# A hand-ordered drain with paired second norms and its own PSUM banks, and weight pieces converted one step sooner

## The reference

```python
h = x.as_patches @ W                                  # (64 images, 36 tokens, 192)
n = layernorm(h)
q, k, v = split(n @ W_attn.T + b_attn)                # 12 heads of 16
att = softmax(where(causal, q @ k.T / 4, -inf))       # 36 x 36 for each image and head
h = h + (att @ v) @ W_o.T + b_o
n = layernorm(h)
probs = softmax(n @ router_w.T)                       # 8 experts
top_w, top_i = top_k(probs, 2); top_w /= top_w.sum()
for e in range(8):                                    # 192 -> 768 -> 192
    h = h + w_e * (gelu(n @ w1[e] + b1[e]) @ w2[e] + b2[e])   # w_e: top_w of the tokens that chose e
```

## Time and profile before

| | us |
|---|---|
| median of three runs | 411.71 (411.45 to 411.98) |
| the profiled execution's own time | 414.29 |
| its span in the trace | 412.5 |
| PE busy in the span | 370.5 (90%) |
| DVE busy | 253.5 (61%) |
| ACT busy | 217.1 (53%) |
| POOL busy | 180.3 (44%) |
| granted TensorE clock, mean | 0.979 of full |

### The profile page before, as it was taken

One profiled execution on the slowest core, in us unless ns is written; L12 is line 12 of the kernel. 1 busy time (PEld: TensorE's weight loads), 2 busy tenths in 40 slices (PEclk: granted clock), 3 DMA queues, 4 the chain that ended last, 5 costly groups with the idle time before them and its releaser, 6 DMA issues.

```text
span 412.5 us, 14891 instructions
## 1 busy us (share of the span) xinstructions
PE 370.5 (90%) x5740; PEld 327.1 (79%) x5740; DVE 253.5 (61%) x656; ACT 217.1 (53%) x443; POOL 180.3 (44%) x219
## 2 busy tenths in 40 slices
PE   3989999989999999997998889999999999999900
PEld 3879989979989899874454589999999999999800
DVE  4696468877877778785298154555445555445425
ACT  5668667778787786853233144444444444444300
POOL 8116322246455452317308545555555555553300
PEclk9999999999999999999999999999999999999965
DMA  8974004433344333361151213121223222121167
GB/s 255 311 252 150 15 21 127 134 87 102 97 119 116 81 86 92 109 186 32 51 130 50 59 31 89 55 86 57 80 61 88 80 60 84 55 58 42 38 254 274
DMA packets 29705, 42.82 MB, mean 104 GB/s; under 512 B 12416, under 2 KB 19440, under 8 KB 29640
## 3 DMA queue, kind: packets, MB, share of 16 engines
q1 hardware_dynamic: 25512, 33.37, 26.9%
q0 software_dynamic: 4128, 8.50, 7.4%
HBM read 30.23 MB, written 9.67 MB: 97 GB/s over the span
## 4 chain that ended last, share of the span: by engine, by line
PE 41%; issue 6%; DVE 5%; POOL 3%; DMA 3%; ACT 1%; SPq 0%; POOLq 0%; DVEq 0%
PE PSA L1259 19%; PE PSA L1274 15%; PE PSA L1137 3%; DMA W2h<-yrows 3%; POOL XF L477 2%; PE PSA L1278 2%; PE PSA L1226 2%; DVE PTR L938 1%; DVE H L1000 1%; POOL REG L484 1%; DMA yrows<-KBR 1%; DVE VB L935 1%; POOL REG L483 1%; PE PSA L1204 0%; SPq L444 0%
## 5 line engine op out<-in xcount | busy, mean ns | idle before, releaser
L1259 PE MATMUL PSA<-YT,W1h 128*128 128x128 f16 x774 | 78.0, 219 | 2.4 <-DVE YT L962 2.4
L1259 PE MATMUL PSA<-YT,W1l 128*128 128x128 f16 (+1 forms) x516 | 75.3, 220 | 0.0
L1274 PE MATMUL PSA<-W2h,PTR 128*128 x516 | 71.0, 246 | 0.3 <-DVE PTR L699 0.3
L516 POOL DMA_INDIRECT yrows<-KBR x43 | 43.0, 999 | 63.5 <-DVE KBR L977 63.2
L1259 PEld LDWEIGHTS PSA<-YT,W1h 128*128 x774 | 63.7, 98 | 6.6 <-DVE YT L962 2.8
L685 ACT ACTIVATE PTR<-PSA 128x768 f32<-128x768 f32 x43 | 34.8, 810 | 57.6 <-PE PSA L1259 52.7
L1274 PE MATMUL PSA<-W2l,PTR 128*128 x258 | 63.5, 246 | 0.0
L699 DVE SCALAR_TENSOR_TENSOR PTR<-PTR 128x768 f16<-128x768 f32 x43 | 41.2, 958 | 26.6 <-issue 14.2
L690 ACT ACTIVATE PTR<-PTR 128x768 f16<-128x768 f32 x43 | 36.3, 843 | 40.3 <-PE PSA L1278 40.1
L511 POOL DMA_INDIRECT REG<-xrows,KBR x43 | 42.6, 992 | 19.3 <-issue 11.6
L977 DVE TENSOR_SCALAR KBR<-PSA,KBR 128x192 f32<-128x192 f32 x43 | 18.0, 418 | 52.2 <-PE PSA L1278 52.2
(11 more groups left out here) (165 smaller groups left out, 805.6 us busy)
## 6 DMA issues: line engine op xcount, KB each, us to landing
WSTG<-w SPq DMA_DIRECT2D x16, 384.0 KB, 3.6
WSTG<-w SPq DMA_DIRECT2D x16, 336.0 KB, 3.2
REG<-xt SPq DMA_DIRECT2D x12, 324.0 KB, 5.4
W1l<-xt SPq DMA_DIRECT2D x10, 324.0 KB, 6.8
VB<-VP SPq DMA_DIRECT2D x99, 19.1 KB
H<-hrows SPq DMA_DIRECT2D x6, 288.0 KB
xrows<-REG SPq DMA_DIRECT2D x2, 800.2 KB
hrows<-H SPq DMA_DIRECT2D x1, 1296.0 KB
```

The costliest lines, as they stand in the source:

```text
L516: gp.indirect_dma_start(out=yrows, out_offset=bass.IndirectOffsetOnAxis(ap=TARGET[:, s:s + 1], axis=0), in_=YO[s % 2], in_offset=None).the ...
L1259: ins = nc.tensor.matmul(bank(2 * u + f // (FC // 2), 128, FC // 2 * ST_)[:, w:w + ST_], weights[a, c], YT[0:rows, at:at + ST_], start=k = ...
L1274: nc.tensor.matmul(bank(4 + u, ST_, C), GP[a][:, at:at + ST_], weights[b], start=(f, a, b) == (0, 0, 0), stop=False)
```

## The change

The expert weights' schedule and the pipeline's end are rewritten.

- `pieces(i)` becomes `range(3 * (i + 1) // 2, 3 * (i + 2) // 2)`: the first piece's high part now comes in step -1, inside the embedding, and even steps have two and odd steps one. DVE's low parts, a step behind, are one at even i and two at odd i. The last piece's low part stands in front of `shift(21)`.
- The loop of steps ends at tile 20 (`range(NT - 1)`). What follows is written out by hand on PE, ACT, DVE and POOL.
- The second norms of tiles 16 to 21 go in three pairs: one ACT instruction for the high parts of two tiles (`pair_hi`), two for the low parts (`pair_low` on POOL, `last_low` on DVE for the last pair), six transposes (`pair_transpose`), one eviction of 648 columns (`pair_out`), ten router matmuls (`pair_router`) and one copy of the logits (`pair_logits`). The rows of tiles 16 and 17 are still normalised by POOL; those of 18 to 21 by DVE (`late_rows`).
- Banks: the pairs' transposes use PSUM banks 0 and 2, the late router results bank 3, and the projection of tile 20 bank 5. Pair 18 uses the first norm's buffer `XF[0]`.
- SP stores the residual rows as soon as they are computed (`h2_done`) and no longer behind the normalised rows (`n2_row`).
- The unread matmuls of the end are dealt out anew. In the embedding PE's steps are `early(i)`, with the same instructions as `step(i)` had there.

Its core (the first-line declarations, the helper `pair_rows`, which views two tiles' rows, and the router's waits are left out):

```diff
+        def pair_source(t):
+            return XF[1] if t != PAIRS[1][0] else XF[0]
+
+        def pair_bank(t):
+            return 2 if t == PAIRS[1][0] else 0
...
         def pieces(i):
-            return range(max(0, 3 * i // 2), min(2 * PIECES, 3 * (i + 1) // 2))
-
-        FIRST_NORM, GROUP, DRAIN = 8, 4, 3
+            return range(max(0, 3 * (i + 1) // 2), max(0, min(2 * PIECES, 3 * (i + 2) // 2)))
+
+        FIRST_NORM, GROUP = 8, 4
+        PAIRED = NT - 6
+        PAIRS = [(t, t + 1) for t in range(PAIRED, NT, 2)]
...
         def norm2_at(i):
-            at = {t: t + 5 for t in range(NT)}
-            at.update({t: NT - 1 + (t - (NT - 6)) // 2 for t in range(NT - 6, NT)})
-            return [t for t in range(NT) if at[t] == i]
+            return [i - 5] if 5 <= i < PAIRED + 5 else []
...
+        def project_bank(t):
+            return 5 if t == NT - 2 else 6
+
+        def router_bank(t):
+            return 3 if t >= PAIRED - 1 else 6
...
-                sp.wait_ge(n2_row, b)
+                sp.wait_ge(h2_done, b)
...
-            sp.wait_ge(n2_lo, 2 * NT)
+            sp.wait_ge(n2_lo, 2 * (NT - 2))
+            sp.wait_ge(last_lo, 2)
...
+            def pair_low(t):
+                gp.wait_ge(n2_hi, t + 2)
+                x = pair_source(t).rearrange("p (t c) -> p t c", c=C)
+                nc.gpsimd.tensor_tensor(pair_rows(t, C, CB), x[:, :, CA:C], pair_rows(t, CA, CB), ALU.subtract).then_inc(n2_lo, 2)
+                nc.gpsimd.tensor_tensor(pair_rows(t, LOW_A, CA), x[:, :, 0:CA], pair_rows(t, 0, CA), ALU.subtract).then_inc(n2_lo, 2)
...
+            for t in PAIRS[0]:
+                norm2_row(t)
+            pair_low(PAIRS[0][0])
+            pair_low(PAIRS[1][0])
...
+            def pair_hi(t):
+                if t == PAIRS[0][0]:
+                    act.wait_ge(n2_row, t + 2)
+                else:
+                    act.wait_ge(late_row, t + 2 - PAIRS[1][0])
+                nc.scalar.activation(pair_rows(t, 0, C), pair_source(t).rearrange("p (t c) -> p t c", c=C), ACT.Copy).then_inc(n2_hi, 2)
+
+            def pair_out(t):
+                act.wait_ge(n2_mm, t + 2)
+                act.wait_ge(r_mm, t)
+                nc.scalar.activation(XT[:, :], bank(pair_bank(t), 128, 6 * TT, F16), ACT.Copy).then_inc(n2_done, 2)
+
+            for i in range(NT - 1):
                 step(i)
+            exps(NT - 1)
+            norm2_out(PAIRED - 1)
+            probs_hi(NT - 1)
+            y_hi(NT - 2)
+            inverse_deviation(group(NT - 3))
+            y_hi(NT - 1)
+            pair_hi(PAIRS[0][0])
+            inverse_deviation(group(NT - 1))
+            pair_hi(PAIRS[1][0])
+            pair_out(PAIRS[0][0])
+            pair_hi(PAIRS[2][0])
+            pair_out(PAIRS[1][0])
+            pair_out(PAIRS[2][0])
...
+                if t < NT - 2:
+                    need(dve, o_mm, t + 2)
...
+            def pair_logits(t):
+                dve.wait_ge(r_mm, t + 2)
+                nc.vector.tensor_copy(LG[:, t * E:(t + 2) * E], bank(router_bank(t), TT, 512)[:, ROUT:ROUT + 2 * E]).then_inc(lg_done, 2)
...
+            def late_rows(t):
+                dve.wait_ge(rs_done, group(t) + 1)
+                if t == PAIRS[1][0]:
+                    dve.wait_ge(n1_hi, NT)
+                    dve.wait_ge(n1_lo, NT)
+                else:
+                    dve.wait_ge(n2_hi, t - 2)
+                    dve.wait_ge(n2_lo, 2 * (t - 2))
+                for n in range(2):
+                    x = pair_source(t)[:, n * C:(n + 1) * C]
+                    nc.vector.tensor_scalar(x, htile(t + n), MEAN[:, NT + t + n:NT + t + n + 1], RS[:, NT + t + n:NT + t + n + 1],
+                                            ALU.subtract, ALU.mult).then_inc(late_row, 1)
+
+            def last_low(t):
+                dve.wait_ge(n2_hi, t + 2)
+                x = pair_source(t).rearrange("p (t c) -> p t c", c=C)
+                nc.vector.tensor_tensor(pair_rows(t, C, CB), x[:, :, CA:C], pair_rows(t, CA, CB), ALU.subtract).then_inc(last_lo, 1)
+                nc.vector.tensor_tensor(pair_rows(t, LOW_A, CA), x[:, :, 0:CA], pair_rows(t, 0, CA), ALU.subtract).then_inc(last_lo, 1)
...
+            for n in pieces(NT - 2):
+                piece_lo(n)
+            shift(NT - 1)
+            residual(NT - 3)
+            outputs(NT - 2)
+            stats2(NT - 3)
+            probs_lo(NT - 1)
+            logits(PAIRED - 1)
+            y_lo(NT - 2)
+            variances(group(NT - 3))
+            outputs(NT - 1)
+            refine(group(NT - 3))
+            y_lo(NT - 1)
+            residual(NT - 2)
+            stats2(NT - 2)
+            residual(NT - 1)
+            stats2(NT - 1)
+            variances(group(NT - 1))
+            late_rows(PAIRS[1][0])
+            refine(group(NT - 1))
+            late_rows(PAIRS[2][0])
+            last_low(PAIRS[2][0])
+            for t, _ in PAIRS:
+                pair_logits(t)
...
+            def pair_transpose(t):
+                if t == PAIRS[2][0]:
+                    pe.wait_ge(last_lo, 2)
+                else:
+                    pe.wait_ge(n2_lo, 2 * (t + 2))
+                pe.wait_ge(qh_done, NT)
+                pe.wait_ge(kh_done, 2 * NT)
+                pe.wait_ge(sub_done, NT)
+                if t == PAIRS[2][0]:
+                    pe.wait_ge(n2_done, PAIRS[1][0])
+                for m in range(2):
+                    for n, at in enumerate(BLOCKS):
+                        ins = nc.tensor.transpose(bank(pair_bank(t), 128, 6 * TT, F16)[:, (3 * m + n) * TT:(3 * m + n + 1) * TT],
+                                                  rows2(t + m, at, 128), IDH[0:TT, 0:TT])
+                ins.then_inc(n2_mm, 2)
+
+            def pair_router(t):
+                pe.wait_ge(n2_done, t + 2)
+                pe.wait_ge(lg_done, t)
+                for m in range(2):
+                    for k, (a, c, n) in enumerate(ROUTER_PRODUCTS):
+                        ins = nc.tensor.matmul(bank(router_bank(t), TT, 512)[:, ROUT + m * E:ROUT + (m + 1) * E],
+                                               two(XT, t + m, 3 * TT)[:, n * TT:(n + 1) * TT],
+                                               WR[a][:, c * E:(c + 1) * E], start=k == 0, stop=k == len(ROUTER_PRODUCTS) - 1)
+                ins.then_inc(r_mm, 2)
...
-                late = i > NT - DRAIN
+                late = i == NT - 2
...
+            scores(NT - 1)
+            project(NT - 3)
+            outputs(NT - 2)
+            norm2_transpose(NT - 1, PAIRED - 1)
+            unread(1)
+            transpose_probs(NT - 1)
+            transpose_y(NT - 2)
+            router(NT - 1, PAIRED - 1)
+            unread(3)
+            outputs(NT - 1)
+            project(NT - 2)
+            unread(2)
+            transpose_y(NT - 1)
+            unread(3)
+            project(NT - 1)
+            unread(11)
+            pair_transpose(PAIRS[0][0])
+            unread(4)
+            pair_router(PAIRS[0][0])
+            pair_transpose(PAIRS[1][0])
+            unread(1)
+            pair_transpose(PAIRS[2][0])
+            pair_router(PAIRS[1][0])
+            unread(1)
+            pair_router(PAIRS[2][0])
```

More of the change, by code:

```diff
@@ L405, in _ @@
             sp.wait_ge(consts_set, FILLS)
-            for i in range(-2, NT + 1):
+            for i in range(-2, NT):
                 for n in pieces(i - 1):
@@ L484, in norm2_low @@
                 nc.gpsimd.tensor_tensor(rows2(t, LOW_A, CA), x[:, 0:CA], rows2(t, 0, CA), ALU.subtract).then_inc(n2_lo, 1)
-            for i in range(-6, NT + DRAIN):
+            def pair_low(t):
[3 more added lines that the diff above has]
+                nc.gpsimd.tensor_tensor(pair_rows(t, LOW_A, CA), x[:, :, 0:CA], pair_rows(t, 0, CA), ALU.subtract).then_inc(n2_lo, 2)
+            for i in range(-6, NT):
                 if has(i + 5):
@@ L664, in _ @@
             inverse_deviation(1)
-            for i in range(NT + DRAIN):
-                step(i)
+            def pair_hi(t):
[9 more added lines that the diff above has]
+            for i in range(NT - 1):
+                step(i)
+            exps(NT - 1)
[11 more added lines that the diff above has]
+            pair_out(PAIRS[2][0])
             act.wait_ge(route, 11)
@@ L781, in residual @@
                 need(dve, op_mm, t + 1)
-                need(dve, o_mm, upto(t + 2))
-                nc.vector.scalar_tensor_tensor(htile(t), bank(6, TT, 512)[:, PROJ:PROJ + C], 1 / S_XW, htile(t), ALU.mult, ALU.add).then_inc(h2_done, 1)
+                if t < NT - 2:
+                    need(dve, o_mm, t + 2)
+                nc.vector.scalar_tensor_tensor(htile(t), bank(project_bank(t), TT, 512)[:, PROJ:PROJ + C], 1 / S_XW, htile(t), ALU.mult, ALU.add).then_inc(h2_done, 1)
             def logits(t):
                 need(dve, r_mm, t + 1)
-                nc.vector.tensor_copy(LG[:, t * E:(t + 1) * E], bank(6, TT, 512)[:, ROUT:ROUT + E]).then_inc(lg_done, 1)
```

(39 more changed lines are left out.)

8 lines of the change are left out of this document (5 added, 3 removed).

## The result

The kernel after takes 409.25 us (median of 8 runs, 408.43 to 410.81) against 411.89 for the kernel before beside it (8 runs, 411.39 to 412.30): a ratio of 0.994, 95% interval 0.9923 to 0.9958. It is faster, by 2.6 us and not by the 5.3 of the forecast, and outside the range. Its profiled execution, the fastest of the eight, took 408.43 us, with a span of 406.3 and a mean granted clock of 0.972; six of the other seven have 0.964 to 0.969.

What follows compares the result with a forecast made beforehand. PE bounds the steady pipeline, and the drain is a chain over all engines. A drain gain of 7.7 us less 2.4 for the pieces is 5.3, so 411.7 becomes 406.4 us, range 404.2 to 408.4.

Steps and rivals of the forecast that it cites:

- rival C: In the new drain, PE's waits lower the clock to 1.2 GHz: 4.7 us late, 413 us if twice; chance 0.02.
- Cost: 2.4 us: Pipeline steps with a group's end: DVE's second piece delays `y_lo` and `refine`, PE waits; 0.57 + 0.64 + 0.59 + 0.59 us.
- what ACT gives back with one piece less: Steps 6 and 10: ACT's exponential no longer ends last, which gives back 0.15 us.
- The drain 7.7 us sooner: From the last tile's scores to routing: routing starts at 196.83 instead of 204.49 us.
- this hold: In the drain, DVE and POOL instructions exclude each other: 0 to 0.6 us for `late_rows`, taken as 0 with quicker DVE.
- The prediction's own sign of being wrong: In the profile after, a granted clock that shows anything but full would make the whole prediction wrong.
- no cost in the other odd steps: Pipeline steps without a group's end: two pieces fit on DVE, cost zero.
- none on SP: SP's last piece leaves near 175.6 instead of 176.32 us, with 0.9 us of margin before ACT wants it.
- none in the embedding: The piece in step -1 lies on ACT ahead of an exponential that waits for DVE, which covers it.
- routing and experts as long as before: After the drain, routing and experts were to keep their old lengths.
- A: Rival on the pipeline: the added pieces cost nothing, time 404.0 us; chance 0.10.
- B: Rival on the drain: it gains only 5.3 to 6.3 us, time 408.2 us; chance 0.23.

Runs made afterwards that it cites:

- e1: The kernel before, unchanged, run once more: 411.08 us.
- e4: The kernel after, unchanged, run once more: 408.98 us, ratio 0.9939 to the kernel before.
- e9: The kernel after with eleven filling matmuls added in the drain and three ahead of the projection in steps 6, 10, 14 and 18: ratio 0.9898 to the kernel before.
- e2: The kernel before with only the new body of `pieces`: 413.15 us, ratio 1.0047 to the kernel before.
- e3: The kernel after with two pieces on DVE at even steps and one at odd steps: 406.23 us, ratio 0.9872 to the kernel before.
- e5: e3 with eleven more filling matmuls in the drain: 405.00 us, ratio 0.9842 to the kernel before.
- e8: e5 with ACT's first piece ahead of the second norm's high part in steps with a group's end: 403.37 us, ratio 0.9812 to the kernel before.
- e7: e3 with POOL's low parts of tiles 16 and 17 held until the last variances are computed: 407.24 us.

## Why the prediction was wrong

The step that failed is that the clock was put at nothing. The sum has no term for it, and rival C, which had one, got a chance of 0.02; in the trace of the kernel after it costs 0.9 us in step 6 and 1.0 ahead of the ranks, and most other executions have a lower mean clock still. Beside it two terms were mis-sized: the gain of the drain by 1.0 us too much, and the wait that the pieces make by 1.3 us too much.

The sum of the profile after against e1, a typical trace of before: embedding +0.4, pipeline 131.56 - 129.62 = +1.9, drain 18.78 - 25.41 = -6.6, routing up to the first expert matmul 28.74 - 27.74 = +1.0, experts 0.0, behind them +0.2: -3.1 us, spans 409.4 and 406.3. The +0.4 is no cost of the change: in e4 the first scores come at 48.39 us, sooner than in e1 (48.76).

- **"Cost: 2.4 us", the pieces: mis-sized twice, and the sum came near by luck.** The delays came where and nearly as they were forecast: POOL's part 0.7 to 0.8 us later in steps 6 and 10 and 0.6 in 14 and 18, with waits of PE for `y_lo` of 0.97, 0.65, 0.46 and 0.46 us (0.28 in step 6 before, none in the others). But what ACT gives back with one piece less is 0.41 us in steps 6 and 10 and 0.26 in 14 and 18. I had taken step 14 for one in which ACT does not end last, and it did: from the norm's transposes to those of the probabilities it is 0.99 us before and 0.73 after. So the waits cost 0.2 to 0.3 us each, 1.1 together (e9, and the two executions of e2 with a full clock). On top came 0.8 to 0.9 us for each fall of the clock in the pipeline.
- **"The drain 7.7 us sooner": right in its order, 1.0 us too much.** Up to the statistics of tile 21 each step is within 0.1 us of the forecast. Then 0.55 us for the two small instructions under POOL's low part; I had named this hold and set it to zero. The Trainium skill's page SBUF — State Buffer, section Who interferes with whom, states that a DVE instruction with two SBUF inputs contends with a POOL instruction that reads SBUF, and that whoever holds the shared ports holds them for its whole instruction. The trace agrees for two instructions: L783 ends at 192.29 and L786 at 192.91, with the POOL instructions beside them (192.27 and 192.89). It is less than the prediction worked out by that page, 0.55 us and not 1.7, as the other five of the seven kept their 0.15 to 0.17 us. The other 0.5 lie in hops: 0.1 at the rows, 0.15 in POOL's low parts, 0.1 at each of the last router steps.
- **Rival C, the clock, at 0.02: the step that failed most.** The mean clock is at most 0.973 in all 19 executions of the kernel after, and at least 0.975 in each of the kernel before for which it is on record. In the two traces a fall lasts 3.4 us, once 6.8. Rival C was dismissed by one row: from 188 to 192 us PE had been busy 2.68 of 4 us in the kernel before, at full clock. That comparison held (2.97 of 4 us from 194 to 198 in the new drain), and the clock fell all the same at 199.3. One stretch that kept its clock was no proof for the next. In the pipeline the prediction saw the new waits and asked nothing about the clock there. The price of one fall is 1.0 us in routing, by the mechanism named there (filling that takes twice its time and holds up the ranks), not the 4.7 of a clock that stays low. The prediction's own sign of being wrong, a clock that shows anything but full, was there.
- **The base.** The profiled execution of before (414.29 us) was 2.4 over the median of the eight; against e1 its excess lies among the experts, in the transfer at the end and in the embedding. The difference of profiles, 6.2 us, would have flattered the forecast; that of the medians is 2.6.
- **Right:** no cost in the other odd steps, none on SP, none in the embedding; routing and experts as long as before, but for the clock. The chances of the forecast, A and B add to 0.96, where the prediction says 0.95; nothing hangs on it.

Shown by experiment is that the new waits bring the falls in the pipeline: they are in all three traces with the waits unfilled (after, e4, e2) and in none of the seven without those waits (before, e1, e3, e5 to e8), nor in the one with the waits filled (e9). Open is what makes a fall land in step 6 in one execution and in step 10 in another, and why the drain of e7 had none.

## What to carry to other kernels

When work moves by one step in a software pipeline, look at which steps are already full: here the second piece went into just those with the extra work, and the choice between even and odd steps was worth 2.8 us (e3 against e4). A wait on TensorE can cost itself and what the clock does after it, and not every execution shows it: compare the mean clocks of all executions before trusting one trace. Filling belongs where the engine waits, and as little as possible in front of work that is on the path.

## What was not expected of the hardware

Waits of 0.65 us in an otherwise full pipeline were followed by 3.4 us at 1.2 GHz (step 10 in e2 and e4). Not every one was: the kernel after kept its clock behind the same wait in its step 10, and e4 behind 0.97 us in step 6. With 0.65 us of filling in them, none of the four steps lost the clock in the one trace (e9). A VectorE instruction on two columns took 0.52 us instead of 0.16 with a GpSimd instruction beside it.
